# First stage of an eight-core hybrid kernel: statistics-to-diagonals chain and own-tile normalization moved to GpSimd

## The reference

```python
def _layernorm(x, axis=-1, eps=1e-5):
    m = jnp.mean(x, axis=axis, keepdims=True)
    v = jnp.var(x, axis=axis, keepdims=True)
    return (x - m) / jnp.sqrt(v + eps)

def _L0_attn_a_ref(x, Wq, Wk, Wv):
    Q = jnp.einsum('bti,id->btd', x, Wq)
    K = jnp.einsum('bti,id->btd', x, Wk)
    V = jnp.einsum('bti,id->btd', x, Wv)
    m = jnp.einsum('btd,bt->td', K, V.sum(axis=-1))
    # s_t = gamma * s_(t-1) + m_t over the tokens, reshaped to S
    return S[None, :, :] * Q

x = x + _L0_attn_a_ref(_layernorm(x), L0_attn_a_Wq, L0_attn_a_Wk, L0_attn_a_Wv)
# then a routed FFN, a delta-rule attention with an MLP, and the FFN again
```

## Time and profile before

| What | us |
|---|---|
| median of 3 runs | 1960.49 (1955.18 to 1962.06) |
| the profiled execution, device time | 1966.91 |
| its span on the slowest core (core 4) | 1965.3 |
| spans of all cores | 1940.0 to 1965.3 |
| busy TensorE / VectorE / ScalarE / GpSimd over the span | 1659.0 / 886.8 / 705.6 / 205.8 |

### The profile page before, as it was taken

One profiled execution on the slowest core, in us unless ns is written; L12 is line 12 of the kernel. 1 busy time (PEld: TensorE's weight loads), 2 busy tenths in 40 slices (PEclk: granted clock), 3 DMA queues, 4 the chain that ended last, 5 costly groups with the idle time before them and its releaser, 6 DMA issues.

```text
span 1965.3 us, 23417 instructions; the slowest of 8 cores (1940.0 to 1965.3 us)
## 1 busy us (share of the span) xinstructions
PE 1659.0 (84%) x8118; PEld 791.0 (40%) x8266; DVE 886.8 (45%) x1699; ACT 705.6 (36%) x1066; POOL 205.8 (10%) x256
## 2 busy tenths in 40 slices
PE   2899997832799996898998999999999994289997
PEld 1444443311344443444544444444444442144443
DVE  4799995776122226256433332542222446511222
ACT  4899995238211134301333221430011101622112
POOL 2222221112010013000000000000000000300002
PEclk9999999875899997898999999999999997599999
DMA  8976762590166659800001010680054222173445
GB/s 240 284 238 230 256 232 54 102 192 33 55 103 109 111 133 215 188 1 1 33 12 37 8 43 1 129 139 1 1 87 85 43 44 54 43 244 60 82 86 86
DMA packets 69458, 201.15 MB, mean 102 GB/s; under 512 B 4644, under 2 KB 4708, under 8 KB 69344
## 3 DMA queue, kind: packets, MB, share of 16 engines
q0 software_dynamic: 40960, 94.76, 27.6%
q1 hardware_dynamic: 28384, 104.89, 16.0%
HBM read 228.97 MB, written 33.59 MB: 134 GB/s over the span
## 4 chain that ended last, share of the span: by engine, by line
PE 66%; ACT 10%; DMA 7%; DVE 6%; issue 5%; ACTq 3%; DVEq 1%; SPq 0%; POOL 0%; POOLq 0%
PE v_h1ps L1008 11%; PE v_h2ps L1020 10%; PE mlp_a L1694 6%; PE ab_bank L1529 5%; PE mlp_a L1682 5%; ACT scr_s L432 4%; ACT scr_s L427 3%; PE ab_bank L1567 3%; PE mlp_a L1708 3%; PE ab_bank L1473 3%; PE ab_bank L1423 3%; PE mlp_r L1708 3%; PE ab_big L1454 3%; PE ab_bank L1480 3%; PE ab_bank L1542 2%
## 5 line engine op out<-in xcount | busy, mean ns | idle before, releaser
L513 PE MATMUL yps<-ring,diag 128*128 128x512 f32 x448 | 204.0, 608 | 29.7 <-POOL diag L393 29.7
L1020 PE MATMUL v_h2ps<-m_w,m_h1q 128*128 128x512 bf16 x1000 | 221.1, 379 | 1.3
L1008 PE MATMUL v_h1ps<-m_sel_fm,m_w 128*128 128x512 bf16 x1006 | 221.0, 379 | 0.9
L957 ACT ACTIVATE m_h1q<-v_h1ps,fb_s 128x512 bf16<-128x512 f32 x128 | 87.8, 688 | 294.3 <-PE v_h1ps L1008 294.3
L933 DVE TENSOR_TENSOR m_acc<-v_h2ps,m_acc 128x512 f32<-128x512 f32 x96 | 66.3, 692 | 263.0 <-PE v_h2ps L1020 263.0
L590 DVE SCALAR_TENSOR_TENSOR scr_v<-ring,wvs_bc 128x1024 bf16<-128x1024 f32 x128 | 153.4, 1217 | 0.6 <-DMA ring<-x_all 0.3
L1020 PEld LDWEIGHTS v_h2ps<-m_w,m_h1q 128*128 128x128 bf16 x1024 | 100.2, 98 | 120.8
L1008 PEld LDWEIGHTS v_h1ps<-m_sel_fm,m_w 128*128 128x128 bf16 x1024 | 100.1, 98 | 120.4
L1666 ACT ACTIVATE gate_prod<-mlp_a 128x512 bf16<-128x512 f32 x64 | 38.2, 598 | 272.2 <-PE mlp_a L1682 272.0
L513 PEld LDWEIGHTS yps<-ring,diag 128*128 128x128 f32 x448 | 84.5, 194 | 127.3 <-issue 127.3
L1682 PE MATMUL mlp_a<-xln_fm,wg_buf 128*128 128x512 bf16 x502 | 111.6, 379 | 3.1 <-ACT gate_prod L1666 2.6
(11 more groups left out here) (263 smaller groups left out, 2257.2 us busy)
## 6 DMA issues: line engine op xcount, KB each, us to landing
ring<-x_all SPq DMA_DIRECT2D x64, 1024.0 KB, 7.3
m_w<-fW POOLq DMA_DIRECT2D x16, 2048.0 KB, 15.4
x_tok<-x_all POOLq DMA_DIRECT2D x16, 512.0 KB, 7.7
y_dram<-x_tok SPq DMA_DIRECT2D x4, 2048.0 KB, 23.6
x_tok<-y_dram SPq DMA_DIRECT2D x16, 512.0 KB, 4.3
x_tok<-y_dram POOLq DMA_DIRECT2D x16, 512.0 KB, 5.3
out<-x_tok SPq DMA_DIRECT2D x4, 2048.0 KB, 21.7
m_sel_tok<-sel_dram SPq DMA_DIRECT2D x8, 514.0 KB, 5.9
```

What stands on the lines that cost most here:

```text
L513: ii = t.matmul(yps[tt % 2][:, h * 512:(h + 1) * 512], lhsT=diag_of(n), rhs=x_tile(n)[:, h * 512:(h + 1) * 512], start=(n % B == 0), stop= ...
L957: s.activation(out=h1q[:, ft * D + h * 512:ft * D + (h + 1) * 512], in_=h1ps[n % 4][:, :], func=AF.Gelu_apprx_tanh, bias=fb1_s[:, q * 8 + ...
L1008: ii = t.matmul(h1ps[n % 4][:, :], lhsT=w1[:, dt * D + ft * P:dt * D + (ft + 1) * P], rhs=sel_fm[:, dt * D + h * 512:dt * D + (h + 1) * 51 ...
L1020: ii = t.matmul(h2ps[m % 4][:, :], lhsT=h1q[:, ff * D + rt * P:ff * D + (rt + 1) * P], rhs=w2[:, ff * D + h * 512:ff * D + (h + 1) * 512], ...
```

## The change

GpSimd takes over the chain between statistics and diagonals. VectorE loses `coefs` and `mean_term`; at the end of each group's dot products it signals `a_dots`. GpSimd waits for `a_dots` and `a_stat`, adds eps, and takes the variance to the power -1 (a tensor operation with a constant tile `powers`), and for an even group the own tile's variance also to the power -0.5. The diagonals are now the identity times the dot product times the inverse variance, in one instruction with two column operands; `coef` itself is made after the odd group's diagonals, for `z_scale` and the mean term, and `a_coef` now counts token tiles. The mean term is built in six small steps with a sum by halves and signals `a_nb`, for which `y_finish` now waits; the drain there goes. `own_norm` moves from ScalarE, behind the odd group's statistics, to GpSimd, behind the even group's diagonals, as one instruction (subtract the mean, multiply by the root); its wait for the transposition of the previous own tile (`a_owntr`) goes with it.

```diff
-    [('a_coef', 32), ('ab_pev', 64)],
+    [('a_coef', 16), ('ab_pev', 64)],
+    [('a_dots', 32)],
+    [('a_nb', 16)],
...
-    onmr = b.sb('a_onmr', (P, NT), F32)
-    nmean = b.sb('a_nmean', (P, NT), F32)
+    powers = b.sb('a_powers', (P, 5), F32)
...
+            g.memset(powers[:, 0:4], -1.0)
+            g.memset(powers[:, 4:5], -0.5)
             g.wait_ge(sem('a_wvmm'), at('a_wvmm', 1))
             g.dma_start(out=wq16[:, :].rearrange('p (k n) -> p k n', k=ND),
                         in_=wD['aWq'].rearrange('(k p) n -> p k n', p=P)).then_inc(sem('a_wq'), 16)
+            def roots(gi):
+                c0, tt = 4 * gi, gi // 2
+                g.wait_ge(sem('a_dots'), at('a_dots', gi + 1))
+                g.wait_ge(sem('a_stat'), at('a_stat', gi + 1))
+                g.tensor_scalar(out=inv4[:, 0:4], in0=mv[:, 2 * c0 + 1:2 * c0 + 8:2], scalar1=1e-05, scalar2=None, op0=ALU.add)
+                g.drain()
+                g.tensor_tensor(out=inv8[:, c0:c0 + 4], in0=inv4[:, 0:4], in1=powers[:, 0:4], op=ALU.pow)
+                if gi % 2 == 0:
+                    g.tensor_tensor(out=orst[:, tt:tt + 1], in0=inv4[:, 0:1], in1=powers[:, 4:5], op=ALU.pow)
+                g.drain()
+
+            def own_norm(tt):
+                if tt >= 1:
+                    g.wait_ge(sem('a_owntr'), at('a_owntr', tt))
+                g.drain()
+                g.tensor_scalar(out=ownln[:, :], in0=x_tile(B * tt), scalar1=mv[:, 2 * B * tt:2 * B * tt + 1], scalar2=orst[:, tt:tt + 1],
+                                op0=ALU.subtract, op1=ALU.mult).then_inc(sem('a_ownln'), 1)
+
+            def mean_term(tt):
+                c0 = B * tt
+                g.tensor_tensor(out=coef[:, c0:c0 + B], in0=dotw[:, c0:c0 + B], in1=inv8[:, c0:c0 + B], op=ALU.mult).then_inc(sem('a_coef'), 1)
+                g.drain()
+                g.tensor_tensor(out=aw8[:, 0:B], in0=coef[:, c0:c0 + B], in1=cS['mean_scale'][:, :], op=ALU.mult)
+                g.drain()
+                g.tensor_tensor(out=aw8[:, B:2 * B], in0=mv[:, 2 * c0:2 * c0 + 16:2], in1=aw8[:, 0:B], op=ALU.mult)
+                g.drain()
+                g.tensor_tensor(out=aw8[:, 0:4], in0=aw8[:, B:B + 4], in1=aw8[:, B + 4:B + 8], op=ALU.add)
+                g.drain()
+                g.tensor_tensor(out=aw8[:, 4:6], in0=aw8[:, 0:2], in1=aw8[:, 2:4], op=ALU.add)
+                g.drain()
+                g.tensor_tensor(out=nbias[:, tt:tt + 1], in0=aw8[:, 4:5], in1=aw8[:, 5:6], op=ALU.add).then_inc(sem('a_nb'), 1)
+
             for gi in range(NGRP):
-                g.wait_ge(sem('a_coef'), at('a_coef', gi + 1))
+                roots(gi)
                 for j in range(4):
                     n = 4 * gi + j
                     if n % B >= NPE:
                         continue
                     if gi >= 2 and j % 2 == 0:
                         g.wait_ge(sem('a_ymm'), at('a_ymm', ymm_no(unit_of(n - B))))
-                    g.tensor_scalar(out=diag_of(n), in0=cS['ident32'][:, :], scalar1=coef[:, n:n + 1], scalar2=1.0,
+                    g.tensor_scalar(out=diag_of(n), in0=cS['ident32'][:, :], scalar1=dotw[:, n:n + 1], scalar2=inv8[:, n:n + 1],
                                     op0=ALU.mult, op1=ALU.mult).then_inc(sem('a_diag'), 1)
+                if gi % 2 == 0:
+                    own_norm(gi // 2)
+                else:
+                    mean_term(gi // 2)
             g.wait_ge(sem('a_qmm'), at('a_qmm', NT))
             g.dma_start(out=wk16[:, :].rearrange('p (k n) -> p k n', k=ND),
                         in_=wD['aWk'].rearrange('(k p) n -> p k n', p=P)).then_inc(sem('a_wk'), 16)
...
 
-            def own_norm(tt):
-                s.wait_ge(sem('a_coef'), at('a_coef', 2 * tt + 1))
-                s.activation(out=orst[:, tt:tt + 1], in_=inv8[:, B * tt:B * tt + 1], func=AF.Sqrt)
-                s.drain()
-                s.activation(out=onmr[:, tt:tt + 1], in_=nmean[:, tt:tt + 1], func=AF.Identity, scale=orst[:, tt:tt + 1])
-                s.drain()
-                if tt >= 1:
-                    s.wait_ge(sem('a_owntr'), at('a_owntr', tt))
-                s.activation(out=ownln[:, :], in_=x_tile(B * tt), func=AF.Identity, scale=orst[:, tt:tt + 1],
-                             bias=onmr[:, tt:tt + 1]).then_inc(sem('a_ownln'), 1)
-
             def z_scale(tt):
                 n = B * tt + NPE
-                s.wait_ge(sem('a_coef'), at('a_coef', 2 * tt + 2))
+                s.wait_ge(sem('a_coef'), at('a_coef', tt + 1))
                 if tt >= 2:
                     s.wait_ge(sem('a_ysum'), at('a_ysum', tt - 1))
                 s.activation(out=z_of(tt), in_=x_tile(n), func=AF.Identity, scale=coef[:, n:n + 1]).then_inc(sem('a_z'), 1)
...
                 stats(2 * tt + 1)
-                own_norm(tt)
             z_scale(NT - 1)
             q_evict(NT - 2)
             q_evict(NT - 1)
...
                     t.wait_ge(sem('a_wq'), at('a_wq', 16))
-                    t.wait_ge(sem('a_coef'), at('a_coef', 1))
+                    t.wait_ge(sem('a_dots'), at('a_dots', 1))
                 else:
                     t.wait_ge(sem('a_qev'), at('a_qev', tt))
                 t.wait_ge(sem('a_ownev'), at('a_ownev', tt + 1))
...
                     v.wait_ge(sem(f'a_ld{u % NSLOT}'), at(f'a_ld{u % NSLOT}', 16 * (u // NSLOT + 1)))
-                    v.scalar_tensor_tensor(out=scr_v[:, j % 2 * D:(j % 2 + 1) * D], in0=x_tile(n), scalar=1.0, in1=wvs_bc[:, :],
-                                           op0=ALU.mult, op1=ALU.mult, accum_out=dotw[:, n:n + 1])
+                    ii = v.scalar_tensor_tensor(out=scr_v[:, j % 2 * D:(j % 2 + 1) * D], in0=x_tile(n), scalar=1.0, in1=wvs_bc[:, :],
+                                                op0=ALU.mult, op1=ALU.mult, accum_out=dotw[:, n:n + 1])
                     if 4 * (gi % 2) + j in DVE_STATS:
                         v.bn_stats(sbn[:, 0:6], x_tile(n)[:, 0:512])
                         v.bn_stats(sbn[:, 6:12], x_tile(n)[:, 512:1024])
                     elif j == 1:
                         v.drain()
                         v.bn_aggr(mv[:, 8 * gi:8 * gi + 2], sbn[:, :])
+                ii.then_inc(sem('a_dots'), 1)
                 v.drain()
-
-            def coefs(gi):
-                c0 = 4 * gi
-                v.wait_ge(sem('a_stat'), at('a_stat', gi + 1))
-                v.tensor_scalar(out=inv4[:, 0:4], in0=mv[:, 2 * c0 + 1:2 * c0 + 8:2], scalar1=1e-05, scalar2=None, op0=ALU.add)
-                if gi % 2 == 0:
-                    tt = gi // 2
-                    v.tensor_scalar(out=nmean[:, tt:tt + 1], in0=mv[:, 2 * c0:2 * c0 + 1], scalar1=-1.0, scalar2=None, op0=ALU.mult)
-                v.drain()
-                v.reciprocal(out=inv8[:, c0:c0 + 4], in_=inv4[:, 0:4])
-                v.drain()
-                v.tensor_tensor(out=coef[:, c0:c0 + 4], in0=dotw[:, c0:c0 + 4], in1=inv8[:, c0:c0 + 4],
-                                op=ALU.mult).then_inc(sem('a_coef'), 1)
-                v.drain()
-
-            def mean_term(tt):
-                c0 = B * tt
-                v.tensor_tensor(out=aw8[:, 0:B], in0=coef[:, c0:c0 + B], in1=cS['mean_scale'][:, :], op=ALU.mult)
-                v.drain()
-                v.scalar_tensor_tensor(out=aw8[:, B:2 * B], in0=mv[:, 2 * c0:2 * c0 + 16:2], scalar=1.0, in1=aw8[:, 0:B],
-                                       op0=ALU.mult, op1=ALU.mult, accum_out=nbias[:, tt:tt + 1])
 
             def own_evict(tt):
                 v.wait_ge(sem('a_owntr'), at('a_owntr', tt + 1))
...
                 v.wait_ge(sem('a_z'), at('a_z', tt + 1))
+                v.wait_ge(sem('a_nb'), at('a_nb', tt + 1))
                 if tt >= 1:
                     v.wait_ge(sem('a_ytr'), at('a_ytr', tt))
-                v.drain()
                 for h in range(2):
                     ii = v.scalar_tensor_tensor(out=y16[:, h * 512:(h + 1) * 512], in0=yps[tt % 2][:, h * 512:(h + 1) * 512],
                                                 scalar=nbias[:, tt:tt + 1], in1=z_of(tt)[:, h * 512:(h + 1) * 512], op0=ALU.add, op1=ALU.add)
...
                 tiles(2 * tt)
-                coefs(2 * tt)
                 if tt >= 2:
                     y_evict(tt - 2)
                 tiles(2 * tt + 1)
-                coefs(2 * tt + 1)
-                mean_term(tt)
             y_evict(NT - 2)
             own_evict(NT - 1)
             y_finish(NT - 1)
```

## The result

The changed kernel takes 1990.33 us (median of 4 runs, 1987.48 to 1993.35), the kernel before 1961.28 us (median of 4, 1955.18 to 1965.62). The ratio is 1.0151 with a 95% interval of 1.0126 to 1.0176: **slower by 1.5%**, where 1946.5 us and a range up to 1975 were forecast. The profiled execution took 1993.35 us, its span 1991.7 us on core 4, which is also the core of the rows of before (span 1965.3 us), so the two traces can be laid side by side.

What follows compares the result with a forecast made beforehand. ScalarE set first-stage rounds of 17.72 us; TensorE would, at 16.47. Twelve rounds saving 1.25 (15.0), less 2.4 for late diagonals, plus about 1 at the start: 13.6, say 14, off 1960.49 gives 1946.5 us; range 1942 to 1975.

Steps and rivals of the forecast that it cites:

- All three signs: First stage: dots over 1.36 us every round, TensorE waiting over 0.5 us a round for diagonals, or a power over 1 us.
- TensorE's floor: First-stage round: TensorE's own work without waiting, 16.47 us, would become the bound, saving at most 1.25 us a round.
- The loss to dots: GpSimd's round: 5 to 6 of 19 reading instructions caught by VectorE's dots, adding some 5.7 us.
- The wait for `a_nb`: VectorE's new wait in `y_finish`, in front of two dots; costed at nothing.
- a gain of 1 us at the start: First stage's start: `own_norm` off ScalarE (2.06 us earlier), against the longer chain, brings about 1 us.
- GpSimd's sum: GpSimd's round: 9.0 us of work plus 5.7 behind dots, 14.7 us, still under TensorE's 16.47.
- eleven small steps with their drains: GpSimd's additions, powers and mean-term steps: ten at 0.45 us and the last at 0.35, 4.9 a round.
- The second rival: GpSimd's power is a long software routine; GpSimd becomes the bound and the change loses from 1.0 us more per power; chance 0.2.
- the mild end: Smaller power costs of the second rival, counted within 0.5% of no change; 1.2 us more per power gives 1968 us.
- The first rival: VectorE and GpSimd on the shared SBUF path become the bound, rounds 17.2 to 17.7 us; 1954.5 us at 17.3; chance 0.24.
- Latency: GpSimd's chain from an even group's last dot to first diagonal: some 3 us, hidden within 5.7 us left by TensorE.

Runs made afterwards that it cites:

- e2: Changed kernel with GpSimd's three powers a round replaced by products of the same operands, inverses and roots left out; ratio 1.0005, rounds 16.48 us.
- e3: Changed kernel plus one early power on constants, VectorE's dots replaced by sums over one SBUF input; ratio 1.0008, rounds 16.48 us.
- e8: e5 with addition and reciprocal back on VectorE, GpSimd keeping diagonals, mean term, `own_norm` and one root; median 1950.86 us, ratio 0.9908.
- e5: Changed kernel with every drain of GpSimd's new chain replaced by a semaphore wait for its own step; ratio 1.0050, rounds 18.07 us.
- e7: Kernel before the change with only one GpSimd drain added, ahead of its first diagonal; ratio 1.0064.
- e9: Changed kernel with the load of Wq issued after the first group's diagonals and first `own_norm`; no ratio, profiled execution 1999.27 us.
- e6: e5 with `own_norm` split into pieces of 128, 256 and 640 columns; no ratio, profiled execution 1990.94 us, rounds 19.17 us.
- e4: Changed kernel plus one early power on constants, `own_norm` moved to VectorE between `own_evict` and `y_finish`; ratio 1.0120.

## Why the prediction was wrong

All three signs that the prediction named for being wrong came: dots of 1.89 or 1.97 us in ten of the sixteen rounds, a wait of TensorE of 1.3 us a round, and a power of 1.04 us.

**What was right.** ScalarE set the round; relieved, it needs some 16.0 us and VectorE 15.2 (e2; forecast 15.66 and 15.2), and TensorE's floor is 16.475 us (forecast 16.47), shown by e2, e3 and e8. Where that floor is reached, 13 rounds are 14.9 us shorter than before (229.1 - 214.2); the forecast had 15.0 for twelve. The loss to dots was put at 5.7 us and is 5.4. The wait for `a_nb` costs nothing, the ring's loads land after 7.9 us (7.3 in the earlier trace rows) and hold nobody up.

**The drain: the step that failed most.** The drains behind GpSimd's steps were priced at 0.07 to 0.1 us, from VectorE's dependent steps: one engine's drain was carried to another. In the rounds 0.15 us pass at one, start of the next step included, but 23.1 us at the first one. The queue that the chain was moved to has the load of Wq in it, issued some 9 us earlier and 32.8 us on its way, and the prediction went through the queues of SP but not through GpSimd's own; no rival had a drain in it. Instead of a gain of 1 us at the start there was a loss of 25.4; e5 gives back about 20 us of the result, e7 shows it alone, e9 moves it. Without the drain the first `y_rows` is still 4.9 us late (e5), a loss that the sum did not have either.

**GpSimd's sum: two terms mis-sized.** Per round, forecast against the changed kernel:

| term | forecast, us | measured, us |
|---|---|---|
| seven diagonals | 2.45 | 3.04 |
| eleven small steps with their drains | 4.9 | 4.3 + 1.6 of gaps |
| `own_norm` | 1.7 | 3.79 |
| behind dots | 5.7 | 5.4 |
| sum | 14.7 | 18.1 |

`own_norm` lies above even its upper end, 2.8: the bound was a diagonal of the earlier trace rows times eight. That diagonal multiplied by one column; with two column operands it takes 0.43 from start to start, and `own_norm`'s form takes 0.80 on 128 columns (e6) and 3.3 ns for each further one, so a long diagonal was the wrong stand-in. Nor was 0.23, the time after which a diagonal lets a dot in, a measure of the work: `own_norm` lets a dot in after 1.06 of its 3.79 us (below). The four-column power is 1.04, inside its bounds of 0.35 to 1.57, of which the lower was taken; the one-column root is 0.55. By this sum, with the power at the forecast's price GpSimd's round would be 18.1 - 1.6 = 16.5, with `own_norm` at its price 16.0: either error alone would have left TensorE the bound, or next to it, and the two together made GpSimd the bound. e2, with 2.0 us less, shows the first of these two. The second was not run by itself, and e4, where GpSimd has no `own_norm` at all and rounds still take 17.57 or more, shows that the sum alone does not decide it.

**The second rival**, the power as a long routine, is right in direction (GpSimd bound, slower) and wrong in its place: it needed 1.0 us more per power to lose, and 0.7 for two of the three and 0.2 for the third were enough because `own_norm` took the rest. Rounds of 18.1 without the pause came to 1.0050 (e5, its start 4.9 us late), about what it called the mild end.

**The first rival** (the shared path): its open question, who wins between two dots that follow directly, has no single answer. In the changed kernel four diagonals and four `own_norm` waited through both dots (a diagonal at 91.13 took 2.48 us; the 128-column piece of e6 takes 2.8). Ten powers on four columns and seven diagonals that were issued just before the first dot were let in between: the last diagonal of the four from 191.02 on is one, and the dot behind it, at 193.55, took 1.38. Its own mechanism, `own_norm` holding up VectorE by its whole length, does not happen. Taking 4.54 - 3.79 = 0.75 us as the time that `own_norm` of 194.05 waited for the running dot, it begins in earnest at 194.80; the next dot, started at 195.10, takes 1.97 instead of 1.21 us, so it was let in at about 195.86. That is 1.06 us, of a length of 3.79, and it is 1.05 or 1.06 in all ten rounds in which a dot meets it so. e8 has it without that reckoning: an unhindered `own_norm` of 3.79 starts at 46.42, and a dot that starts at 46.70 takes 1.99, so it was let in at 47.48. In e6 the 640 columns, reckoned alike, keep a dot out for 0.73 us. In e8 a dot that starts 1.87 us into a free `own_norm` has its normal 1.21. The Trainium skill (SBUF — State Buffer, Who interferes with whom) has the shared pair as an exclusive lock, which the one that issues first gets for the whole instruction. For a dot that came first the rows here agree (a diagonal of 0.45 takes 1.55 behind one), for GpSimd's `own_norm` they don't, by the 1.06 of 3.79.

**Latency.** "With TensorE as the bound that is hidden" holds in e2, e3 and e8. The reckoning itself (5.7 us left for a chain of 3) was too short by what dots add between the steps: in e4, by its rows, the chain sets the round though GpSimd stands still in each.

**Still open.** e7 costs 0.64%, while in the profiled executions its stage ends only 9.4 us (0.48% of the span) later than before; the difference is within the interval and was not followed up. Why the drain in front of the first power of e9 lasts 1.31 us and not 0.15 is not known either. Whether the drain waits for the data to land, or for some earlier sign of the load's end that falls within the same 0.2 to 0.8 us, the traces do not tell.
